# Scan stage: delta*u in PSUM, half scans, single-bank filters, and a GpSimd product that waits for its own state's scan alone

## Chip, cores and metric

The kernel runs on one core of a Trainium2 chip. The metric is the device time of one execution in microseconds (us), as the median of the runs.

## The reference

The network takes x of 16 sequences x 512 tokens x 128 features through six residual blocks: a mixture of experts, attention, two more mixtures, a selective state-space block, and a last mixture. The change touches the state-space block alone. Cut to what matters:

```python
xz = einsum('bld,ed->bel', h, W_in);  x, z = xz[:, :256], xz[:, 256:]
xc = gate[0] * silu(conv(x, w1, dil=1) + b1) + gate[1] * silu(conv(x, w2, dil=2) + b2)   # 4 taps each, causal
dt_low, B, C = split(W_x @ xc, [64, 16, 16])
delta = softplus(W_dt @ dt_low + b_dt);  A = -exp(A_log)             # A: 256 x 16 states
h_t = h_{t-1} * exp(delta_t * A) + delta_t * B_t * xc_t              # 512 steps, 256 x 16 states
y_t = sum over n of h_t[:, n] * C_t[n] + D * xc_t
out = W_out @ (y * silu(z))
```

## The kernel before

The kernel is a row of stages, with a barrier between them: load, routing, expert blocks (four times in all), attention, and `scan_stage` between the last two mixtures. Everything is float32 unless a row says bf16. X, all 8192 tokens, stays in SBUF throughout.

`scan_stage` goes through 16 sequences, and in each through NB = 16 states n. The 256 inner features lie as DT = 2 tiles of 128 partitions, so that one state is a tile of 128 x 1024 (2 x 512 time steps). Each engine runs a program of its own, written by hand: `run` calls `main(s, b, n)` and then `between(s, b, turn, n)` for each state. main is the recurrence of sequence s. between spreads the work of the neighbours over the states: the gating, the output projection, the residual and the routing of sequence s-1, the convolutions and step sizes of s+1, and the taking and the norm of s+2. Each engine executes its queue in order; semaphores (`wait_ge`) are the only ties.

For one state:
- ScalarE (`decay`) writes dA = exp(delta * A[n]) by two activations of 128 x 511 into a ring of RA = 4. In step n it makes state n+1.
- VectorE multiplies ux = delta*xc by the broadcast row B of the state, half by half (L1543, "mult A", and L1546, "mult B"), from SBUF into PSUM tile psX of three banks: even states use banks 0 and 1, odd ones 2 and 1, which is why the halves change places, (dt + n) % DT. Then one `tensor_tensor_scan` (L1552) runs over both halves, 1024 elements; the first dA of each half is 0 and so separates them. It writes H, a ring of RH = 4.
- GpSimd (L1484) multiplies H by the broadcast row C, both from SBUF, into HC, a ring of RP = 4. It waits for the scan of its state (h_ready), for both mults of the *next* state (dBx_done), and for TensorE to be done with the HC of three states before. For n < 8 it then issues one indirect DMA (L369) of a routed row block of sequence s-2.
- TensorE (`total`, L1310) adds HC to psY with an identity matmul, in step n+2.

On VectorE, between has after the scan of n = 1 the gating (L1529, one input in PSUM), after n = 3 the residual sum (L1534, one input in PSUM) and norm statistics (L148 to L158), after n = 5 the norm's end (L174 to L251), after n = 6 the sum and statistics of s+2 (L488, L148 to L156), after n = 9 their end (L174 to L181), after n = 10 the router's top (L299, L300) and `mix` (L1510), after n = 12 the router's choice (L315 to L328), after n = 14 the router's places (L345 to L349) and `step_sizes_1` (L1516), and after n = 15 `step_sizes_2` (L1520, L1521, L1523: delta and ux). Small operations in chains wait for the one before through semaphore `linked`.

TensorE's between has the convolutions of s+1 (`conv`, each 4 taps, g = 0 to 5) in PSUM tile psA of two banks, cut over steps 1 to 7 by CONV_STEPS, then `project` (n = 10) and `steps` (n = 12). ScalarE empties psA (`empty`), runs `silu` in n = 8 with two table loads, `to_low` in n = 11 and `soften` (softplus) in n = 13. SyncE writes the B and C rows to DRAM and loads them back broadcast, two states to a transfer, in four slots that wait for H*C.

PSUM: psA 2 banks, psX 3, psR 1, psY 2, all eight.

Of the kernel before, what the change touches and what calls it, by code (L numbers as in the profile page):

```python
# [19 lines left out]
P = 128  # L20
# [831 lines left out]
def attention_stage(nc, k, wqkv, source):  # L852


    with Stage(nc, "att") as st:
# [231 lines left out]
        def _(dve):  # L1087
# [37 lines left out]
            def body(s, b, turn, first, last):  # L1125
# [41 lines left out]
CONV_STEPS = {1: ((0, (0, 1)),), 2: ((0, (2, 3)),), 3: ((1, (0, 1, 2)),), 4: ((1, (3,)), (2, (0, 1))), 5: ((2, (2, 3)), (3, (0,))),  # L1167
              6: ((3, (1, 2, 3)),), 7: ((4, (0,)), (5, (0,)))}
EMPTY_STEPS = {2: (0,), 4: (1,), 5: (2,), 7: (3,), 8: (4, 5)}


def scan_stage(nc, k, source):
# [4 lines left out]
    with Stage(nc, "ssm") as st:  # L1177
# [6 lines left out]
        zs, xc, delta, ux = (sb(n, [P, 2, DT, SEQ]) for n in ("zs", "xc", "delta", "ux"))  # L1184
# [4 lines left out]
        ST, NB = SEQ_TILES, STATES  # L1189
        CHUNK, SLOTS = 2, 4  # L1190
# [3 lines left out]
        psA, psX = pb("psA", [P, 2, SEQ]), pb("psX", [P, DT + 1, SEQ])  # L1194
# [6 lines left out]
        dA_ready, dBx_done, h_ready, hc_ready, y_summed, y_ready, out_summed, added, cleared, z_done = map(  # L1201
            sem, "dA_ready dBx_done h_ready hc_ready y_summed y_ready out_summed added cleared z_done".split())
# [48 lines left out]
        def _(pe):  # L1251
            def flip(s):
                pe.wait_ge(normed, s + 1)
                if positive(s):
                    pe.wait_ge(v_ready, s)
                for j in range(ST):
                    last = nc.tensor.transpose(psA[:, 1, j * P:(j + 1) * P], xn[:, j, :], k.ident[:, :])
                last.then_inc(flipped, 1)

            def conv(s, g, taps=range(TAPS)):  # L1260

                c, dt = g // 2, g % 2
                o = psA[:, g % 2, :]
                if 0 in taps:
                    if g == 0:
                        pe.wait_ge(turned, s + 1)
                    if g >= 2:
                        pe.wait_ge(emptied, s * 6 + g - 1)
                if g < 2 * DT:
                    for t in taps:  # L1270
                        back = (TAPS - 1 - t) * (c + 1)
                        last = nc.tensor.matmul(o, Wtap[:, c, t, dt * P:(dt + 1) * P], hT[:, PAD - back:PAD - back + SEQ], start=(t == 0), stop=(t == TAPS - 1))  # L1272
                    done = TAPS - 1 in taps
                else:
                    last = nc.tensor.matmul(o, Win[:, INNER + dt * P:INNER + (dt + 1) * P], hT[:, PAD:PAD + SEQ], start=True, stop=True)
                    done = True
                if done:
                    last.then_inc(fronted, 1)
# [76 lines left out]
            steps(0)  # L1355
# [12 lines left out]
        def _(act):  # L1368
            def to_hT(s):
                act.wait_ge(flipped, s + 1)  # L1370
                nc.scalar.activation(hT[:, PAD:], psA[:, 1, :], ACT.Copy).then_inc(turned, 1)  # L1371

            def empty(s, b, g):
                c, dt = g // 2, g % 2
                act.wait_ge(fronted, s * 6 + g + 1)
                if g < 4:
                    nc.scalar.activation(pre[:, g, :], psA[:, g % 2, :], ACT.Identity, bias=col[:, dt, c:c + 1]).then_inc(emptied, 1)  # L1377
                else:
                    nc.scalar.activation(zs[:, b, dt, :], psA[:, g % 2, :], ACT.Copy).then_inc(emptied, 1)
# [10 lines left out]
            def to_low(s):  # L1390
# [309 lines left out]
```

## Time and profile before

| | us |
|---|---|
| median of 3 runs | 3390.18 (3386.60 to 3391.48) |
| the profiled execution | 3394.06 |
| its span in the profile | 3390.8 |
| scan stage in that span | about 1749 to 3012 |

Over the span TensorE is busy 2470.6 us (73%), VectorE 2227.6 (66%), GpSimd 1685.4 (50%) and ScalarE 1604.3 (47%). These shares mix stages with different limits, so the scan stage has to be read by itself. In a table of groups a line gives the source line, engine, operation, output <- inputs and shapes, the count, the busy time and the mean of one, and behind the bar the idle time in front and what ended it. In a list in order of time each line has start, duration (us), engine, source line and operation, and in brackets the idle time in front.

### The profile page before, as it was taken

Reading aid. Unit: us, or ns where it says so; the run is one execution under the profiler, and the core shown is the slowest. Engines: PE = TensorE matmul, PEld = TensorE weight load, DVE = VectorE, ACT = ScalarE, POOL = GpSimd, SP = SyncE. Lnnn points to the kernel's source line nnn. Section 1 sums busy time; section 2 is a strip of 40 time slices with the busy share of each in tenths; the row PEclk is TensorE's granted clock in tenths of the full one; section 3 lists DMA queues with packets and bytes.
Section 4 is the critical chain, followed back from the end, with each engine's and each line's share of the span. In section 5 each row is a group of like instructions: output and inputs, shape, how many; then the busy total and the mean of one; then the engine's idle time right before and its main releaser. Section 6 shows DMA issues by size and latency. Waiting matters only on the chain. (4 is left out here: it accounts for less than half of the span.)

```text
span 3390.8 us, 50612 instructions
## 1 busy us (share of the span) xinstructions
PE 2470.6 (73%) x12640; PEld 1752.9 (52%) x12640; DVE 2227.6 (66%) x6132; ACT 1604.3 (47%) x3126; POOL 1685.4 (50%) x1350
## 2 busy tenths in 40 slices
PE   2419995776499854499867777777777788739992
PEld 2319994555499833399723333333333333319992
DVE  3604445777444455255449999999999999974553
ACT  2205554454255433255445555555555555525551
POOL 2755550443455437555414555555555565654551
PEclk9999997777699976699978888888888888879996
DMA  8137871110478632477523333343333333317876
GB/s 289 52 99 229 226 209 47 54 57 28 120 229 226 175 105 85 132 229 226 167 88 112 120 123 113 118 133 113 125 113 113 125 118 116 120 57 231 225 228 177
DMA packets 268799, 478.94 MB, mean 141 GB/s; under 512 B 37453, under 2 KB 181803, under 8 KB 268560
## 3 DMA queue, kind: packets, MB, share of 16 engines
q1 hardware_dynamic: 208864, 388.64, 38.8%
q0 software_dynamic: 34816, 68.00, 5.6%
q10 hardware_dynamic: 25008, 21.11, 1.8%
q8 instruction: 35, 0.57, 0.1%
q14 instruction: 76, 0.62, 0.1%
HBM read 383.22 MB, written 98.54 MB: 142 GB/s over the span
## 5 line engine op out<-in xcount | busy, mean ns | idle before, releaser
L1484 POOL TENSOR_TENSOR ssm_HC<-ssm_H,ssm_BC 128x1024 f32<-128x1024 f32 x256 | 601.6, 2350 | 579.9 <-DVE ssm_psX L1546 532.3
L1310 PE MATMUL ssm_psY<-ssm_HC,ident 128*128 128x512 f32 x1024 | 555.1, 673 | 202.1 <-POOL ssm_HC L1484 201.5
L1552 DVE TENSOR_TENSOR_SCAN ssm_H<-ssm_dA,ssm_psX 128x1024 f32<-128x1024 f32 x256 | 585.3, 2286 | 44.7 <-issue 31.6
L1310 PEld LDWEIGHTS ssm_psY<-ssm_HC,ident 128*128 128x128 f32 x1024 | 205.1, 210 | 500.5 <-POOL ssm_HC L1484 272.9
L1419 ACT ACTIVATE ssm_dA<-ssm_delta,A 128x511 f32<-128x511 f32 x512 | 329.7, 708 | 102.9 <-DVE ssm_delta L1521 100.4
L369 POOL DMA_INDIRECT xslots<-att_r_xn,att_r_idx x128 | 127.9, 1000 | 246.5 <-DVE att_r_idx L349 210.4
L1272 PE MATMUL ssm_psA<-ssm_hT,Wtap 128*128 128x512 f32 x512 | 244.9, 613 | 2.5 <-ACT ssm_hT L1371 2.5
L768 POOL DMA_INDIRECT b_back<-b_yr,b_to_row x144 | 139.9, 972 | 151.1 <-DVE b_yr L843 129.2
L768 POOL DMA_INDIRECT a_back<-a_yr,a_to_row x144 | 139.9, 971 | 150.4 <-DVE a_yr L843 128.5
L768 POOL DMA_INDIRECT d_back<-d_yr,d_to_row x144 | 139.9, 972 | 148.6 <-DVE d_yr L843 126.7
L768 POOL DMA_INDIRECT c_back<-c_yr,c_to_row x144 | 139.9, 972 | 144.6 <-DVE c_yr L843 122.7
L1377 ACT ACTIVATE ssm_pre<-ssm_psA,col 128x512 f32<-128x512 f32 x64 | 43.7, 684 | 331.6 <-PE ssm_psA L1272 331.6
L1543 DVE TENSOR_TENSOR ssm_psX<-ssm_ux,ssm_BC 128x512 f32<-128x512 f32 x256 | 191.3, 747 | 9.2 <-issue 7.6
L812 ACT ACTIVATE d_H<-d_psH,d_W 128x256 f32<-128x256 f32 x288 | 127.5, 474 | 125.7 <-PE d_psH L789 125.7
L812 ACT ACTIVATE b_H<-b_psH,b_W 128x256 f32<-128x256 f32 x288 | 127.5, 474 | 125.4 <-PE b_psH L789 125.4
L812 ACT ACTIVATE c_H<-c_psH,c_W 128x256 f32<-128x256 f32 x288 | 127.5, 474 | 125.4 <-PE c_psH L789 125.4
L812 ACT ACTIVATE a_H<-a_psH,a_W 128x256 f32<-128x256 f32 x288 | 127.5, 474 | 124.7 <-PE a_psH L789 124.7
L812 ACT ACT_TABLE_LOAD x72 | 92.4, 1283 | 186.3 <-PEq L104 185.1
L1546 DVE TENSOR_TENSOR ssm_psX<-ssm_ux,ssm_BC 128x512 f32<-128x512 f32 x256 | 176.3, 689 | 0.0
L369 POOL DMA_INDIRECT xslots<-to_a_r_xn,to_a_r_idx x128 | 125.6, 981 | 97.6 <-DVE to_a_r_idx L349 56.6
L369 POOL DMA_INDIRECT xslots<-to_c_r_xn,to_c_r_idx x128 | 126.1, 985 | 90.6 <-DVE to_c_r_idx L349 49.8
L1272 PEld LDWEIGHTS ssm_psA<-ssm_hT,Wtap 128*128 128x128 f32 x512 | 101.9, 202 | 131.2 <-issue 127.9
(515 smaller groups left out, 5778.4 us busy)
## 6 DMA issues: line engine op xcount, KB each, us to landing
ssm_BC<-bc_rows SPq DMA_DIRECT2D x128, 1024.0 KB
a_W<-in_l_pack SPq DMA_DIRECT2D x72, 514.0 KB
b_W<-in_l_pack SPq DMA_DIRECT2D x72, 514.0 KB
c_W<-in_l_pack SPq DMA_DIRECT2D x72, 514.0 KB
d_W<-in_l_pack SPq DMA_DIRECT2D x72, 514.0 KB
a_xs<-xslots SPq DMA_DIRECT2D x72, 131.0 KB
b_xs<-xslots SPq DMA_DIRECT2D x72, 131.0 KB
c_xs<-xslots SPq DMA_DIRECT2D x72, 131.0 KB
```

What stands on the lines that cost most here:

```text
L369: pool.indirect_dma_start(out=self.k.xslots[:, :], out_offset=bass.IndirectOffsetOnAxis(ap=self.ids(s, b)[:, i:i + 1].bitcast(U32), axis=0 ...
L768: pool.indirect_dma_start(out=target[:, :], out_offset=bass.IndirectOffsetOnAxis(ap=to_row[:, q, s:s + 1].bitcast(U32), axis=0), in_=yr[:, ...
L812: nc.scalar.activation(H[:, b, f, :], psH[:, f, 0:BLOCK], gelu, bias=W[:, q, HIDDEN + FT * D + f:HIDDEN + FT * D + f + 1]).then_inc(h_read ...
L1272: last = nc.tensor.matmul(o, Wtap[:, c, t, dt * P:(dt + 1) * P], hT[:, PAD - back:PAD - back + SEQ], start=(t == 0), stop=(t == TAPS - 1))
L1310: last = nc.tensor.matmul(psY[:, dt, :], k.ident[:, :], HC[:, n % RP, (dt + n) % DT, :], start=False, stop=(n == NB - 1))
L1377: nc.scalar.activation(pre[:, g, :], psA[:, g % 2, :], ACT.Identity, bias=col[:, dt, c:c + 1]).then_inc(emptied, 1)
L1419: last = nc.scalar.activation(dA[:, n % RA, (dt + n) % DT, 1:], delta[:, b, dt, 1:], ACT.Exp, scale=A[:, dt, n:n + 1])
L1484: nc.gpsimd.tensor_tensor(HC[:, n % RP, :, :], H[:, n % RH, :, :], BC[:, n // CHUNK % SLOTS, 1, n % CHUNK:n % CHUNK + 1, :].to_broadcast([ ...
L1543: nc.vector.tensor_tensor(psX[:, 2 * odd, :], ux[:, b, 0, :], BC[:, c % SLOTS, 0, n % CHUNK, :], ALU.mult)
L1546: nc.vector.tensor_tensor(psX[:, 1, :], ux[:, b, 1, :], BC[:, c % SLOTS, 0, n % CHUNK, :], ALU.mult).then_inc(dBx_done, 1)
L1552: nc.vector.tensor_tensor_scan(flat(H[:, n % RH, :, :]), flat(dA[:, n % RA, :, :]), flat(psX[:, odd:odd + DT, :]), 0.0, ALU.mult, ALU.add) ...
```

## The change

1. `ux` moves from SBUF (two buffers) to PSUM (one, two banks). It is written for s+1 after n = 15, when the mults of s are done.
2. psX has two banks in place of three, and the halves no longer change places. Each half has a scan of its own of 512 elements, into its half of H. Scan A waits for mult A (new semaphore dBx_half), scan B for mult B. The next mult A waits for scan A (h_half), the next mult B for scan B.
3. GpSimd's H*C no longer waits for the mults of the next state.
4. psA has one bank in place of two. Each conv is whole in its step (g in step g+1) and waits for ScalarE to have emptied the one before; ScalarE empties g in step g+2. `steps` runs as two matmuls in n = 11 and 12, the second waiting for ScalarE's Relu of the first half, and `soften` in n = 12.
5. ScalarE makes dA two states ahead in place of one.
6. The taking of s+2 moves: TensorE's part from n = 4 to 0, VectorE's sum and statistics from n = 6 to 2. `out` of s-1 (TensorE, n = 2) waits for that sum, since both use psR.
7. The product with the diagonal D moves from the front of `total` (n = 0) to n = SKIP = 9.

```diff
-CONV_STEPS = {1: ((0, (0, 1)),), 2: ((0, (2, 3)),), 3: ((1, (0, 1, 2)),), 4: ((1, (3,)), (2, (0, 1))), 5: ((2, (2, 3)), (3, (0,))),
-              6: ((3, (1, 2, 3)),), 7: ((4, (0,)), (5, (0,)))}
-EMPTY_STEPS = {2: (0,), 4: (1,), 5: (2,), 7: (3,), 8: (4, 5)}
+CONV_STEPS = {1: 0, 2: 1, 3: 2, 4: 3, 5: 4, 6: 5}
+EMPTY_STEPS = {n + 1: g for n, g in CONV_STEPS.items()}
...
-        psA, psX = pb("psA", [P, 2, SEQ]), pb("psX", [P, DT + 1, SEQ])
+        psA, psX, ux = pb("psA", [P, SEQ]), pb("psX", [P, DT, SEQ]), pb("ux", [P, DT, SEQ])
...
+            def steps(s, dt):
+                if dt == 0:
+                    pe.wait_ge(low_ready, s + 1)
+                else:
+                    pe.wait_ge(v_half, s + 1)
+                nc.tensor.matmul(psA[:, :], Wdt[:, dt * P:(dt + 1) * P], low[0:RANK, :], start=True, stop=True).then_inc(dt_summed, 1)
 
             def out(s):
                 pe.wait_ge(y_ready, s + 1)
+                if there(s, 3):
+                    pe.wait_ge(G.taken, s + 4)
...
-                if n == 0:
-                    if positive(s):
-                        pe.wait_ge(y_ready, s)
+                if n == 0 and positive(s):
+                    pe.wait_ge(y_ready, s)
+                if n == SKIP:
                     for dt in range(DT):
-                        nc.tensor.matmul(psY[:, dt, :], diag[:, dt, :], xc[:, b, dt, :], start=True, stop=False)
+                        nc.tensor.matmul(psY[:, dt, :], diag[:, dt, :], xc[:, b, dt, :], start=False, stop=False)
...
             def soften(s):
-                act.wait_ge(dt_summed, s + 1)
...
+                    act.wait_ge(dt_summed, s * DT + dt + 1)
+                    nc.scalar.activation(absv[:, dt, :], psA[:, :], ACT.Abs, bias=col[:, dt, 2:3]).then_inc(abs_ready, 1)
+                    nc.scalar.activation(v[:, dt, :], psA[:, :], ACT.Relu, bias=col[:, dt, 2:3]).then_inc(v_half if dt == 0 else v_ready, 1)
...
             def main(s, b, n):
-                if n + 1 < NB:
-                    decay(s, b, n + 1)
+                if n + 2 < NB:
+                    decay(s, b, n + 2)
                 elif there(s, 1):
-                    decay(s + 1, 1 - b, 0)
+                    decay(s + 1, 1 - b, n + 2 - NB)
...
                 pool.wait_ge(h_ready, s * NB + n + 1)
-                if n + 1 < NB or there(s, 1):
-                    pool.wait_ge(dBx_done, s * NB + n + 2)
...
-                nc.vector.tensor_tensor(ux[:, b, :, :], delta[:, b, :, :], xc[:, b, :, :], ALU.mult).then_inc(ux_ready, 1)
+                if positive(s):
+                    dve.wait_ge(dBx_done, s * NB)
+                nc.vector.tensor_tensor(ux[:, :, :], delta[:, b, :, :], xc[:, b, :, :], ALU.mult).then_inc(ux_ready, 1)
...
-                odd = n % 2
-                nc.vector.tensor_tensor(psX[:, 2 * odd, :], ux[:, b, 0, :], BC[:, c % SLOTS, 0, n % CHUNK, :], ALU.mult)
+                if positive(s * NB + n):
+                    dve.wait_ge(h_half, s * NB + n)
+                nc.vector.tensor_tensor(psX[:, 0, :], ux[:, 0, :], BC[:, c % SLOTS, 0, n % CHUNK, :], ALU.mult).then_inc(dBx_half, 1)
                 if positive(s * NB + n):
                     dve.wait_ge(h_ready, s * NB + n)
-                nc.vector.tensor_tensor(psX[:, 1, :], ux[:, b, 1, :], BC[:, c % SLOTS, 0, n % CHUNK, :], ALU.mult).then_inc(dBx_done, 1)
-                dve.wait_ge(dBx_done, s * NB + n + 1)
+                nc.vector.tensor_tensor(psX[:, 1, :], ux[:, 1, :], BC[:, c % SLOTS, 0, n % CHUNK, :], ALU.mult).then_inc(dBx_done, 1)
+                dve.wait_ge(dBx_half, s * NB + n + 1)
                 dve.wait_ge(dA_ready, s * NB + n + 1)
                 if positive(s * NB + n - RH + 1):
                     dve.wait_ge(hc_ready, s * NB + n - RH + 1)
-                flat = lambda v: v.rearrange("p a t -> p (a t)")
-                nc.vector.tensor_tensor_scan(flat(H[:, n % RH, :, :]), flat(dA[:, n % RA, :, :]), flat(psX[:, odd:odd + DT, :]), 0.0, ALU.mult, ALU.add).then_inc(h_ready, 1)
+                nc.vector.tensor_tensor_scan(H[:, n % RH, 0, :], dA[:, n % RA, 0, :], psX[:, 0, :], 0.0, ALU.mult, ALU.add).then_inc(h_half, 1)
+                dve.wait_ge(dBx_done, s * NB + n + 1)
+                nc.vector.tensor_tensor_scan(H[:, n % RH, 1, :], dA[:, n % RA, 1, :], psX[:, 1, :], 0.0, ALU.mult, ALU.add).then_inc(h_ready, 1)
```

## Rows read from the trace of the kernel before

**Rows 1.** Busy time of each engine in a stretch: the scan stage.
```profile
core 0: us, PE busy (x) PEld busy (x) DVE busy (x) ACT busy (x) POOL busy (x), PEclk, DMA share, GB/s
1749.00:3012.00 1263.00, 970.67 (x2494) 424.48 (x2494) 1176.05 (x1729) 698.03 (x1110) 731.83 (x371) 0.87 0.34 116
```

**Rows 2.** Groups by line, scan stage: VectorE's scan and mult A, GpSimd's H*C.
```profile
L1552 DVE TENSOR_TENSOR_SCAN ssm_H<-ssm_dA,ssm_psX 128x1024 f32<-128x1024 f32 x256 | 585.3, 2286 | 44.7 <-issue 31.6 <-ACT ssm_dA L1419 1.8 <-DVE ssm_psX L1546 0.5
L1543 DVE TENSOR_TENSOR ssm_psX<-ssm_ux,ssm_BC 128x512 f32<-128x512 f32 x256 | 191.3, 747 | 9.2 <-issue 7.6 <-DVE ssm_ux L1523 0.2
...
L1484 POOL TENSOR_TENSOR ssm_HC<-ssm_H,ssm_BC 128x1024 f32<-128x1024 f32 x256 | 601.6, 2350 | 579.9 <-DVE ssm_psX L1546 532.3 <-issue 38.3 <-PE ssm_psY L1310 7.7
```

**Rows 3.** Waits, scan stage: who waited for whom; total us, times, longest.
```profile
POOL ssm_HC L1484 <- DVE ssm_psX L1546: 532.3, 175, 74.4
...
DVE ssm_H L1552 <- issue: 31.6, 17, 3.7
...
DVE ssm_v L1529 <- PE ssm_psY L1310: 9.3, 16, 4.5
```

**Rows 4.** VectorE in order of time: one state and the next mult A.
```profile
2401.60 0.69 DVE L1543 TENSOR_TENSOR ssm_psX<-ssm_ux,ssm_BC 128x512 f32<-128x512 f32 x1
2402.20 0.69 DVE L1546 TENSOR_TENSOR ssm_psX<-ssm_ux,ssm_BC 128x512 f32<-128x512 f32 x1
2402.93 2.29 DVE L1552 TENSOR_TENSOR_SCAN ssm_H<-ssm_dA,ssm_psX 128x1024 f32<-128x1024 f32 x1
2405.13 0.76 DVE L1543 TENSOR_TENSOR ssm_psX<-ssm_ux,ssm_BC 128x512 f32<-128x512 f32 x1
```

**Rows 5.** VectorE in order of time after the scan of n = 5.
```profile
2408.73 0.47 DVE L174 SCALAR_TENSOR_TENSOR ssm_r_newton<-ssm_r_root 128x8 f32<-128x8 f32 x1
2409.23 0.17 DVE L175 TENSOR_TENSOR ssm_r_newton<-ssm_r_newton,ssm_r_shifted 128x8 f32<-128x8 f32 x1
...
2409.90 0.42 DVE L248 TENSOR_SCALAR ssm_r_rstd<-ssm_r_rstd 128x4 f32<-128x4 f32 x1
```

**Rows 6.** GpSimd in order of time, beside rows 4 and 5.
```profile
2402.98 2.34 POOL L1484 TENSOR_TENSOR ssm_HC<-ssm_H,ssm_BC 128x1024 f32<-128x1024 f32 x1 [2.46 <-DVE ssm_psX L1546]
...
2406.79 2.37 POOL L1484 TENSOR_TENSOR ssm_HC<-ssm_H,ssm_BC 128x1024 f32<-128x1024 f32 x1
2409.32 1.01 POOL L369 DMA_INDIRECT xslots<-ssm_r_xn,ssm_r_idx  x1 [0.16 <-issue]
```

**Rows 7.** In order of time: GpSimd's H*C and VectorE's residual sum beside it.
```profile
2396.99 2.36 POOL L1484 TENSOR_TENSOR ssm_HC<-ssm_H,ssm_BC 128x1024 f32<-128x1024 f32 x1
...
2398.93 0.66 DVE L1534 TENSOR_TENSOR X<-X,ssm_psR 128x512 f32 x1
```

**Rows 8.** One line's instructions, ns min/median/max: L174 and L1484.
```profile
L174 DVE SCALAR_TENSOR_TENSOR ssm_r_newton<-ssm_r_root x16: 167/460/467, 1850.8 to 3018.1; 128x8 f32<-128x8 f32 x16
...
L1484 POOL TENSOR_TENSOR ssm_HC<-ssm_H,ssm_BC x256: 2332/2349/2377, 1755.7 to 3006.8; 128x1024 f32<-128x1024 f32 x128
```

**Rows 9.** VectorE in order of time after n = 3, n = 14 and n = 15.
```profile
2400.64 0.17 DVE L150 TENSOR_TENSOR ssm_r_mean<-ssm_r_stats 128x4 f32<-128x4 f32 x1
...
2400.99 0.17 DVE L153 TENSOR_SCALAR ssm_r_mean<-ssm_r_mean 128x4 f32<-128x4 f32 x1
...
2452.24 0.20 DVE L345 TENSOR_TENSOR ssm_r_pos<-ssm_psR,ssm_r_run 128x64 f32<-128x64 f32 x1
...
2452.57 0.21 DVE L347 TENSOR_TENSOR ssm_r_pos<-ssm_r_pos,ssm_r_hot 128x64 f32<-128x64 f32 x1
...
2457.94 1.26 DVE L1520 TENSOR_TENSOR ssm_rest<-ssm_pre,ssm_rest 128x1024 f32<-128x1024 f32 x1
2459.24 1.23 DVE L1521 TENSOR_TENSOR ssm_delta<-ssm_rest,ssm_v 128x1024 f32<-128x1024 f32 x1
```

**Rows 10.** ScalarE in order of time: the decays behind the silu block.
```profile
2429.77 2.54 ACT L1419 ACTIVATE ssm_dA<-ssm_delta,A 128x511 f32<-128x511 f32 x4
```

**Rows 11.** Groups by line, VectorE after the last state: a scan of 8.
```profile
L404 DVE TENSOR_TENSOR_SCAN ssm_r_end<-ssm_r_ones,ssm_r_nblk 128x8 f32<-128x8 f32 x1 | 0.2, 175 | 0.0
```

**Rows 12.** TensorE in order of time: a part of the convs, and totals after a wait.
```profile
2411.34 2.74 PE L1272 MATMUL ssm_psA<-ssm_hT,Wtap 128*128 128x512 f32 x6
...
2448.90 5.56 PE L1310 MATMUL ssm_psY<-ssm_HC,ident 128*128 128x512 f32 x8 [2.45 <-POOL ssm_HC L1484]
```

More of the change, by code:

```diff
@@ L1256, in flip, with conv @@
                 for j in range(ST):
[L1257 removed]
+                    last = nc.tensor.transpose(psA[:, j * P:(j + 1) * P], xn[:, j, :], k.ident[:, :])
                 last.then_inc(flipped, 1)
[L1260 removed]
+            def conv(s, g):
                 c, dt = g // 2, g % 2
[L1263 to L1268, printed above, removed]
+                if g == 0:
+                    pe.wait_ge(turned, s + 1)
+                else:
+                    pe.wait_ge(emptied, s * 6 + g)
                 if g < 2 * DT:
[L1270 removed]
+                    for t in range(TAPS):
                         back = (TAPS - 1 - t) * (c + 1)
[L1272 to L1278 removed]
+                        last = nc.tensor.matmul(psA[:, :], Wtap[:, c, t, dt * P:(dt + 1) * P], hT[:, PAD - back:PAD - back + SEQ], start=(t == 0), stop=(t == TAPS - 1))
+                else:
+                    last = nc.tensor.matmul(psA[:, :], Win[:, INNER + dt * P:INNER + (dt + 1) * P], hT[:, PAD:PAD + SEQ], start=True, stop=True)
+                last.then_inc(fronted, 1)
             def project(s, b):
@@ L1325, in between @@
                     if n == 7:
-                        if there(s, 2):
-                            pe.wait_ge(G.taken, s + 3)
+                        pe.wait_ge(added, s)
                         R.pe_1a(nc, pe, s - 1, 1 - b)
@@ L1333, in between @@
                 if there(s, 1):
-                    for g, taps in CONV_STEPS.get(n, ()):
-                        conv(s + 1, g, taps)
+                    if n in CONV_STEPS:
+                        conv(s + 1, CONV_STEPS[n])
                     if n == 10:
                         project(s + 1, 1 - b)
+                    if n == 11:
+                        steps(s + 1, 0)
                     if n == 12:
-                        steps(s + 1)
+                        steps(s + 1, 1)
                 if there(s, 2):
-                    if n == 4:
-                        if there(s, -1):
-                            pe.wait_ge(added, s)
+                    if n == 0:
+                        if there(s, -2):
+                            pe.wait_ge(R.rowed, s - 1)
                         G.pe(nc, pe, s + 2, b, turn + 1, psR)
@@ L1370, in to_hT @@
                 act.wait_ge(flipped, s + 1)
-                nc.scalar.activation(hT[:, PAD:], psA[:, 1, :], ACT.Copy).then_inc(turned, 1)
+                nc.scalar.activation(hT[:, PAD:], psA[:, :], ACT.Copy).then_inc(turned, 1)
             def empty(s, b, g):
@@ L1438, in between @@
                 if there(s, 1):
-                    for g in EMPTY_STEPS.get(n, ()):
-                        empty(s + 1, 1 - b, g)
+                    if n in EMPTY_STEPS:
+                        empty(s + 1, 1 - b, EMPTY_STEPS[n])
                     if n == 0:
```

40 lines of the change are left out of this document (17 added, 23 removed).

## Prediction

> **What bounds the kernel now.** I read the busy table by stretch first, then the groups by line, then the waits, then single instructions in order of time. In the scan stage (1749 to 3012 us) VectorE is busy 1176 of 1263 us, TensorE 971, GpSimd 732, ScalarE 698 [rows 1]. VectorE's own idle there is small: 31.6 us before 17 scans ("issue"; behind them, a late dA from ScalarE) and 9.3 us before 16 gated multiplies [rows 3]. So the stage is as long as VectorE's queue, and the change counts by what it does to that queue. GpSimd's H*C idles 532 us, nearly all of it in the wait that the change removes [rows 3]; that idle costs nothing by itself. The other stages are not touched.
>
> One state n costs VectorE 0.60 us from mult A (L1543) to mult B (L1546), 0.73 to the scan (L1552), 2.20 to the next instruction: 3.53 [rows 4]. The 0.73 holds a drain: the scan waits for mult B, which ended at 2402.89. Next instructions otherwise start about 0.09 before the last one's end.
>
> **The fact on which all turns.** Before, GpSimd's H*C (2.35 us, and none of 256 shorter than 2.33 or longer than 2.38 [rows 2, 8]) starts when mult B of the next state has ended, and so runs beside a scan. Where it ran over the scan's end, the VectorE instruction behind was held. At 2408.73 the 128x8 L174 (two inputs in SBUF) took 0.47 us instead of the 0.17 of its neighbour L175, and ended at 2409.20; the H*C beside it ended at 2406.79 + 2.37 = 2409.16 [rows 5, 6]. Its median over 16 sequences is 0.460 [rows 8]. The same H*C tails lift mult A to a mean of 0.747 [rows 2]. On the other hand L1534, with one input in PSUM, started at 2398.93 with the H*C of 2396.99 still running to 2399.35, and took 0.66 [rows 7]; and the scans (dA in SBUF, psX in PSUM) run beside H*C throughout. So in this trace H*C holds back VectorE instructions with both inputs in SBUF and no others. The longest hold seen is about 0.3 us, since by design none of them starts earlier under an H*C. That it would be the whole rest of an H*C is my step beyond the rows. For it: the held L174 got nothing done until the H*C was over (it ended 0.04 us after it), and in 256 H*C none gave way by as much as 0.03 us. GpSimd's indirect DMA holds a third kind: tensor_scalar L248, 0.42 us, ended 2410.32, the DMA at 2410.33 [rows 5, 6].
>
> The Trainium skill ("SBUF — State Buffer", section "Who interferes with whom") says the same of the kinds and more of the length: VectorE with two SBUF inputs and a GpSimd instruction that reads SBUF exclude each other, and whoever is first keeps the port for its whole instruction. The kinds and the tails agree, with L174's 0.47 us; the length of a whole instruction no row here shows. By the rule the sum comes out as the forecast below, by the tails alone as rival 1.
>
> **The change, part by part.**
>
> *ux in PSUM, free mults.* With ux in PSUM, mult A and B have one SBUF input and should pass H*C like L1534. This removes 0.747 - 0.690 = 0.057 us per state.
>
> *Half scans.* Scan A waits for mult A alone, so the drain behind mult B goes: 0.73 becomes 0.60, -0.13. Two scans cost one more fixed part. A scan of 8 elements takes 0.175 [rows 11], one of 1024 2.286 [rows 2]: 2.08 ns an element and 0.16 fixed, so a half is 1.22 and, less the overlap of 0.09, 1.13; twice is 2.27 against 2.20: +0.07. Per state -0.057 - 0.13 + 0.07 = -0.12; x256 = **-31 us**. A mult from PSUM to PSUM isn't in the trace. Bounds: no added cost for the second scan (-0.19, -49 us) to a full fixed part of 0.175 for it and for a slower PSUM mult, with nothing gained (+0.30, +77 us). I take -31, since L1534's 0.66 is nearest.
>
> *dA two states ahead.* dA of a state behind the silu block is the first half of the pair of decays that starts at 2429.77 [rows 10] and is done 1.27 later, at 2431.04, when the waiting scan starts (one of the 17 of rows 3). One more state of lead (3.5 us) covers the 1.6 us of each of 15 waits: **-25 us**, leaving the start of the stage. Soften moves from n=13 to 12 and has its chain through one bank, TensorE waiting for Relu and ScalarE for TensorE; its results are wanted at n=14 and 15, so I cost it at nothing; were the cover gone, one matmul pair and one activation, some 1.5 us a sequence, 25 us.
>
> *TensorE.* Convs at n=1 to 4 are whole: 8 records of 0.43 (six took 2.74 with the last one's tail) = 3.44, with total 1.72, 5.2 us a step [rows 12], against VectorE's 3.5 plus what stands between. At n=2, out now waits for the dve_sum of n=2 (G.taken); total(1) and the convs queue behind it. total(n-2) is wanted only by H*C of n+1 at the earliest and that by a scan three later, so lag of two or three states is hidden: nothing. diag at n=9 rather than n=0 is the same work. SP's loads follow H*C, which comes earlier, not later: nothing.
>
> *H*C free.* This is the large term. H*C now starts about 0.09 after its own scan's end (as 2402.98 follows 2402.89), and so 0.18 after the first instruction that stands between this state and the next starts. What stands there (between) has both inputs in SBUF in 8 of 16 places, and was run in peace before. If a held instruction waits to the H*C's end:
> - n=9: L174 is in front, H*C slips in behind it and L175 waits nearly 2.35. n=5 the same. 2.35 each.
> - n=14: L347 starts 0.33 after the first, so 2.35 - (0.33 - 0.18) = 2.20 is left [rows 9]. n=10 (mix L1510) and n=12 (L316) lie between 2.20 and 2.35. n=15: H*C begins when L1520 ends, L1521 waits 2.35 [rows 9]. These four: 9.1.
> - n=2 and n=3: L150 comes 1.71 after the PSUM sum (2398.93 to 2400.64): 2.35 - (1.71 - 0.18) = 0.82 left. Then the indirect DMA (0.16 later, 1.01 long) meets tensor_scalar L153, 0.35 after L150: again 0.82 [rows 6, 7, 9]. 1.64 each.
>
> With 15 sequences for n=3, 5, 10, 12, 14, 15 and 14 for n=2 and 9: 15 x (1.64 + 2.35 + 9.1) + 14 x (1.64 + 2.35) = 196 + 56 = **+252 us**. Gone in return are the old tails before L174, 32 x 0.30 = **-9**, and about half of the gated wait, **-4**.
>
> Sum: -31 - 25 - 9 - 4 + 252 = **+183 us**. Profiled span 3390.8 gives 3574; that execution took 3394.1, 3.9 over the median of 3390.2, so the median to be expected is **3573 us**.
>
> **The rivals.**
> 1. *The hold is only a tail, or VectorE keeps ahead* (no whole-instruction hold; or H*C doesn't get in between chained instructions, whose gaps are 0.03 to 0.05 us). For: no row shows a hold over 0.4 us. Against: each held instruction ended with the H*C, and no H*C was ever lengthened. Then the 252 is about 0 and the time is 3390 - 69 = **3321 us**, faster. The point from which it decides: the gains of 69 us over 15 x 6 + 14 x 2 = 118 places are 0.58 us a place; with shorter holds than that the kernel is faster. Chance 0.15.
> 2. *A part of it*: the short chained instructions keep H*C out and only the two places with long ones (n=10, 15) are held, 15 x 4.6 = 69, or half of all holds come, 126: 3321 + 69 to 126 = **3390 to 3447**. Chance 0.10.
> 3. *TensorE becomes the bound, beside the holds.* From n=1 to 4 it has 4 x 3.44 of convs, three totals of 1.72 and some 1.9 of out: 21 us at full clock, against 24 of VectorE with its holds. But the granted clock averages 0.87 [rows 1], and after a wait eight records took 5.56 instead of 3.44 [rows 12]. At that pace the 21 become 34, 10 too many; the ring of four H*C hides three states, 10 us, so it decides only where the lag has begun before. If half of the 10 comes through, 15 x 5 = 75: **3648**. Chance 0.06.
> 4. The forecast: holds in full, **3573**. Chance 0.69. Its own range is 3510 to 3640: a quarter of the holds less on the one side; on the other a third of the +108 us that the upper state bound lies above the value taken, and the 25 of soften.
>
> The range is 3400 to 3640: it leaves out rivals 1 and 3. About 0.2% (7 us) is what can be told from no change: faster 0.17, same 0.03, slower 0.80.
>
> **What would show it.** Right: L175 at n=5 and 9, L316 or L317, L347, L1510, L1521 with durations or idle near 2.4 us that end with an H*C; mult A at 0.69 with an H*C running; mult A, mult B, scan A and scan B spaced 0.60, 0.60, 1.13 and 1.13; a sequence 11 to 12 us longer; VectorE still the longest queue; the wait of scan 10 gone. Wrong: those instructions at 0.2 us beside a running H*C; or mults stretched beside it (then ux in PSUM doesn't free them, and the time is over 3640); or scans waiting for dA or hc_ready, which would name ScalarE or TensorE.

## The result, and the profile after

| | before | after |
|---|---|---|
| median, us | 3390.67 (4 runs) | 3532.39 (4 runs, 3530.83 to 3534.42) |
| ratio | | 1.0421, 95% interval 1.0403 to 1.0439 |
| span of the profiled execution | 3390.8 | 3529.0 |
| scan stage, from the start of the first H*C to that of the last gated multiply | 1255.5 | 1391.1 |

The kernel is 142 us slower; 183 were forecast. Nearly all of it is in the scan stage: 1391.1 - 1255.5 = 135.6 of the 138.2 us of the span. The executions come from several chips, and the kernel before takes 3501 to 3538 us on some of them. What is longer there lies outside the scan stage: the kernel of the first experiment below has a stage of 1199.9 us on one chip and 1198.6 on another, and 2292.2 and 2136.7 us outside it; why, no run tells. So below I give the ratio to the kernel before on the same chip, and the length of the scan stage as in the last line of the table. Each stage length is read from one trace; the two pairs of traces of one kernel (1199.9 and 1198.6, 1391.1 and 1390.7) differ by up to 1.3 us, so less than that can't be told from nothing.

The busy time of each engine over the stage, after (columns as in rows 1):

```profile
1749.00:3152.00 1403.00, 1003.66 (x2495) 433.57 (x2496) 1350.51 (x2001) 708.54 (x1112) 733.38 (x373) 0.86 0.31 105
```

VectorE is busy 1350.5 of 1403 us, against 1176.1 of 1263 [rows 1]. It is still the bound, and what grew is its busy time, not its idle time: an instruction that is held counts as busy. The groups by line, VectorE, scan stage (count, busy us, mean ns; behind the bar the idle time before):

```profile
L1551 DVE TENSOR_TENSOR_SCAN ssm_H<-ssm_dA,ssm_psX 128x512 f32<-128x512 f32 x255 | 308.3, 1209 | 0.8 <-issue 0.8
L1553 DVE TENSOR_TENSOR_SCAN ssm_H<-ssm_dA,ssm_psX 128x512 f32<-128x512 f32 x255 | 304.3, 1193 | 0.0
L1543 DVE TENSOR_TENSOR ssm_psX<-ssm_ux,ssm_BC 128x512 f32<-128x512 f32 x255 | 178.5, 700 | 18.3 <-issue 16.3 <-DVE ssm_ux L1522 1.4
...
L1518 DVE TENSOR_TENSOR ssm_delta<-ssm_rest,ssm_v 128x1024 f32<-128x1024 f32 x15 | 48.7, 3245 | 0.5
L1507 DVE SCALAR_TENSOR_TENSOR ssm_xc<-ssm_pre,gates,ssm_xc 128x1024 f32<-128x1024 f32 x15 | 47.2, 3148 | 0.0
L316 DVE TENSOR_TENSOR ssm_r_work<-ssm_r_prob,ssm_r_pv 128x32 f32<-128x32 f32 x30 | 38.3, 1276 | 1.0
L175 DVE TENSOR_TENSOR ssm_r_newton<-ssm_r_newton,ssm_r_shifted 128x8 f32<-128x8 f32 x15 | 37.6, 2507 | 0.5
L347 DVE TENSOR_TENSOR ssm_r_pos<-ssm_r_pos,ssm_r_hot 128x64 f32<-128x64 f32 x15 | 34.0, 2270 | 0.0
L175 DVE TENSOR_TENSOR ssm_n_newton<-ssm_n_newton,ssm_n_shifted 128x4 f32<-128x4 f32 x14 | 33.0, 2357 | 0.5
...
L150 DVE TENSOR_TENSOR ssm_r_mean<-ssm_r_stats 128x4 f32<-128x4 f32 x15 | 12.7, 850 | 0.5
L150 DVE TENSOR_TENSOR ssm_n_mean<-ssm_n_stats 128x4 f32<-128x4 f32 x14 | 11.8, 840 | 0.5
```

Nearly all of the growth is at the places that the prediction named. L175 multiplies 128 x 8 numbers and takes 2.51 us, where its neighbours take 0.17. Above what each takes when nothing holds it (1.225 for L1518, 1.274 for L1507, 0.192 for L316, 0.167 and 0.162 for L175, 0.215 for L347, 0.166 for L150), the eight lines from L1518 down lost 30.3 + 28.1 + 32.5 + 35.1 + 30.8 + 30.7 + 10.3 + 9.4 = 207 us, and L158, L251 and L1513, which it had not named, another 5 or so: 212 us.

One such place in order of time, VectorE and then GpSimd, after n = 9 (start, duration in us):

```profile
2410.85 0.13 DVE L174 SCALAR_TENSOR_TENSOR ssm_n_newton<-ssm_n_root 128x4 f32<-128x4 f32 x1
2411.02 2.36 DVE L175 TENSOR_TENSOR ssm_n_newton<-ssm_n_newton,ssm_n_shifted 128x4 f32<-128x4 f32 x1
2413.41 0.16 DVE L176 SCALAR_TENSOR_TENSOR ssm_n_rstd<-ssm_n_newton,ssm_n_root 128x4 f32<-128x4 f32 x1
...
2411.01 2.35 POOL L1481 TENSOR_TENSOR ssm_HC<-ssm_H,ssm_BC 128x1024 f32<-128x1024 f32 x1 [0.76 <-DVE ssm_H L1553]
```

H*C comes 0.03 us after L174's end, in the gap of the chain, and L175 ends at 2413.38, 0.02 after the H*C. (At n = 5 an indirect DMA runs in front of the H*C, and L175 starts 0.13 us before the H*C does; it is held all the same, for 2.50 to 2.53 us, and for 2.36 in the one sequence that has no DMA there.) Compare rows 5 and 6, where L174 was held for the last 0.3 us of an H*C only. After n = 15 it also goes the other way:

```profile
2447.32 1.20 DVE L1517 TENSOR_TENSOR ssm_rest<-ssm_pre,ssm_rest 128x1024 f32<-128x1024 f32 x1
2448.55 3.25 DVE L1518 TENSOR_TENSOR ssm_delta<-ssm_rest,ssm_v 128x1024 f32<-128x1024 f32 x1
...
2447.48 3.24 POOL L1481 TENSOR_TENSOR ssm_HC<-ssm_H,ssm_BC 128x1024 f32<-128x1024 f32 x1 [5.31 <-DVE ssm_H L1553]
```

L1517 was first, and the H*C takes 3.24 us instead of 2.35 since it has to wait for L1517; then L1518 waits for the H*C.

A state with nothing behind it, VectorE; with rows 4 beside it one sees the half scans and the free mults:

```profile
2400.60 0.67 DVE L1543 TENSOR_TENSOR ssm_psX<-ssm_ux,ssm_BC 128x512 f32<-128x512 f32 x1
2401.18 0.68 DVE L1546 TENSOR_TENSOR ssm_psX<-ssm_ux,ssm_BC 128x512 f32<-128x512 f32 x1
2401.78 1.21 DVE L1551 TENSOR_TENSOR_SCAN ssm_H<-ssm_dA,ssm_psX 128x512 f32<-128x512 f32 x1
2402.91 1.19 DVE L1553 TENSOR_TENSOR_SCAN ssm_H<-ssm_dA,ssm_psX 128x512 f32<-128x512 f32 x1
2404.02 0.67 DVE L1543 TENSOR_TENSOR ssm_psX<-ssm_ux,ssm_BC 128x512 f32<-128x512 f32 x1
...
2400.77 2.35 POOL L1481 TENSOR_TENSOR ssm_HC<-ssm_H,ssm_BC 128x1024 f32<-128x1024 f32 x1 [3.49 <-DVE ssm_H L1553]
```

The spacings are 0.58, 0.60, 1.13 and 1.11, together 3.42, with an H*C running beside mult B and most of mult A.

### The profile page after: what moved, and what is told of

The parts are those of the page before. It is cut to its first block and busy times, and to the rows that moved or that the text cites. A ratio compares the mean times of both kernels' runs of the same rounds, so it can differ in the third digit from the quotient of the medians.

```text
span 3529.0 us, 51026 instructions
## 1 busy us (share of the span) xinstructions
PE 2505.1 (71%) x12640; PEld 1759.0 (50%) x12640; DVE 2398.8 (68%) x6388; ACT 1614.5 (46%) x3126; POOL 1683.9 (48%) x1350
## 5 line engine op out<-in xcount | busy, mean ns | idle before, releaser
L1481 POOL TENSOR_TENSOR ssm_HC<-ssm_H,ssm_BC 128x1024 f32<-128x1024 f32 x256 | 616.6, 2409 | 720.2 <-DVE ssm_H L1553 711.0
L1551 DVE TENSOR_TENSOR_SCAN ssm_H<-ssm_dA,ssm_psX 128x512 f32<-128x512 f32 x256 | 309.5, 1209 | 2.6 <-ACT ssm_dA L1416 1.8
L1553 DVE TENSOR_TENSOR_SCAN ssm_H<-ssm_dA,ssm_psX 128x512 f32<-128x512 f32 x256 | 305.5, 1193 | 0.0
L1543 DVE TENSOR_TENSOR ssm_psX<-ssm_ux,ssm_BC 128x512 f32<-128x512 f32 x256 | 179.2, 700 | 18.3 <-issue 16.3
L1546 DVE TENSOR_TENSOR ssm_psX<-ssm_ux,ssm_BC 128x512 f32<-128x512 f32 x256 | 176.0, 688 | 0.0
```

What stands on the lines that cost most here:

```text
L1481: nc.gpsimd.tensor_tensor(HC[:, n % RP, :, :], H[:, n % RH, :, :], BC[:, n // CHUNK % SLOTS, 1, n % CHUNK:n % CHUNK + 1, :].to_broadcast([ ...
L1543: nc.vector.tensor_tensor(psX[:, 0, :], ux[:, 0, :], BC[:, c % SLOTS, 0, n % CHUNK, :], ALU.mult).then_inc(dBx_half, 1)
L1546: nc.vector.tensor_tensor(psX[:, 1, :], ux[:, 1, :], BC[:, c % SLOTS, 0, n % CHUNK, :], ALU.mult).then_inc(dBx_done, 1)
L1551: nc.vector.tensor_tensor_scan(H[:, n % RH, 0, :], dA[:, n % RA, 0, :], psX[:, 0, :], 0.0, ALU.mult, ALU.add).then_inc(h_half, 1)
L1553: nc.vector.tensor_tensor_scan(H[:, n % RH, 1, :], dA[:, n % RA, 1, :], psX[:, 1, :], 0.0, ALU.mult, ALU.add).then_inc(h_ready, 1)
```

## The experiments

Two theories stood at the start. Theory H: the time goes into holds, as above. Theory T: it goes into TensorE's filters in one bank and its new waits, which the holds only accompany. The next four ran on one chip.

**The wait put back.**

```diff
                 pool.wait_ge(h_ready, s * NB + n + 1)
+                if n + 1 < NB or there(s, 1):
+                    pool.wait_ge(dBx_done, s * NB + n + 2)
```

> The changed kernel with GpSimd's wait for the mults of the next state put back, all else as changed. Theory H (H*C holds VectorE's instructions with two SBUF inputs to its own end): the 212 us that the held instructions lost go, 3532 - 212 = 3320 us, L175 back at 0.17, mix at 1.27, H*C beside the scans. Rival T (the loss comes from TensorE's one-bank filters or from its new waits on the taking of s+2): these are still in, so it stays at 3500 or more.

Measured: 0.9854 of before (0.9838 to 0.9871), stage 1199.9 us: 191 less than the changed kernel, and 56 less than the kernel before. Two more of its lines, VectorE's groups in the scan stage:

```profile
L1545 DVE TENSOR_TENSOR ssm_psX<-ssm_ux,ssm_BC 128x512 f32<-128x512 f32 x254 | 175.1, 689 | 10.3 <-issue 8.2 <-DVE ssm_ux L1524 1.4
...
L174 DVE SCALAR_TENSOR_TENSOR ssm_n_newton<-ssm_n_root 128x4 f32<-128x4 f32 x14 | 10.1, 724 | 0.0
```

Theory T falls: its parts are all still in. The 21 us that are missing from the expected 212 are mostly tails (the last part of an H*C, which runs on past the scan's end and holds the next instruction). They come back with the wait: L174 at n = 9 has a mean of 0.72 in place of 0.14. And the gated multiply waits for TensorE's totals for 13.4 us in all in place of 6.3. The whole account stands in the part on the prediction.

**ux in SBUF, H*C free.**

```diff
+        ux = sb("ux", [P, DT, SEQ])
...
-        psA, psX, ux = pb("psA", [P, SEQ]), pb("psX", [P, DT, SEQ]), pb("ux", [P, DT, SEQ])
+        psA, psX = pb("psA", [P, SEQ]), pb("psX", [P, DT, SEQ])
```

> The changed kernel with ux back in SBUF (one buffer), H*C still free. Theory H: the mults have two SBUF inputs again, so mult A is held after n = 0, 4, 6, 7, 8, 11, 13 by some 2.2 us and after n = 1 by about 1; 16.3 us a sequence more, 3532 + 260 = 3790 us, mult A's mean near 1.7. Rival (the place of ux is nothing to H*C): within 10 us of 3532, mult A near 0.70.

Measured: 3958 us, against 3538 before on that chip (one execution), stage 1672.5 us: 281 more than the changed kernel, 260 expected. VectorE's groups:

```profile
L1547 DVE TENSOR_TENSOR ssm_psX<-ssm_ux,ssm_BC 128x512 f32<-128x512 f32 x255 | 434.5, 1704 | 0.0
...
L1544 DVE TENSOR_TENSOR ssm_psX<-ssm_ux,ssm_BC 128x512 f32<-128x512 f32 x255 | 204.5, 802 | 18.9 <-issue 16.8 <-DVE ssm_ux L1523 1.4
```

The size was right, the place was not: mult B is held (1.70 us), not mult A. Mult A starts 0.09 us before the scan ends and so before H*C can; H*C gets in behind it. So ux in PSUM does what it is for: with a free H*C it is worth 280 us.

**dA two states ahead, alone, in the kernel before.**

```diff
-                if n + 1 < NB:
-                    decay(s, b, n + 1)
+                if n + 2 < NB:
+                    decay(s, b, n + 2)
                 elif there(s, 1):
-                    decay(s + 1, 1 - b, 0)
+                    decay(s + 1, 1 - b, n + 2 - NB)
...
             decay(0, 0, 0)
+            decay(0, 0, 1)
```

> The kernel before with dA made two states ahead, that one part alone. If ScalarE's silu block was what scan 10 waited for: 25 us less, 3365 us, and the idle time before the scans nearly gone. If the late dA has another cause: 3390, with the idle time moved to another n.

Measured: 0.9905 (0.9889 to 0.9922), stage 1224.8: 30.7 us less. The scan's group has 11.4 us of idle time in front, and no "issue" in it, in place of 44.7 with 31.6 [rows 2]:

```profile
L1553 DVE TENSOR_TENSOR_SCAN ssm_H<-ssm_dA,ssm_psX 128x1024 f32<-128x1024 f32 x255 | 583.0, 2286 | 11.4
```

**The wait put back and ux in SBUF** (both edits above).

> The changed kernel with the wait put back and ux in SBUF. Theory H: ux in PSUM is then worth only the tails, since H*C starts behind the mults: 0.057 x 256 = 15 us above the kernel that has the wait alone, 3335 us, mult A at a mean of 0.75. If PSUM as a source has a gain or a price of its own, the two differ by more, or the other way.

Measured: 0.9923 (0.9906 to 0.9939), stage 1222.9. That is 23.0 us more than with the wait alone, where 15 were expected: mult A's mean is 0.804, not 0.75. With half scans the second scan ends 2.23 us after mult B (median; 2.32 in the kernel before), while H*C, which starts 0.13 after mult B's end in both, ends 2.35 later: the tail is longer than it was.

**Half scans alone, in the kernel before.** This and the next three ran on a second chip.

```diff
-                nc.vector.tensor_tensor(psX[:, 2 * odd, :], ux[:, b, 0, :], BC[:, c % SLOTS, 0, n % CHUNK, :], ALU.mult)
+                nc.vector.tensor_tensor(psX[:, 2 * odd, :], ux[:, b, 0, :], BC[:, c % SLOTS, 0, n % CHUNK, :], ALU.mult).then_inc(dBx_half, 1)
...
-                dve.wait_ge(dBx_done, s * NB + n + 1)
+                dve.wait_ge(dBx_half, s * NB + n + 1)
...
-                flat = lambda v: v.rearrange("p a t -> p (a t)")
-                nc.vector.tensor_tensor_scan(flat(H[:, n % RH, :, :]), flat(dA[:, n % RA, :, :]), flat(psX[:, odd:odd + DT, :]), 0.0, ALU.mult, ALU.add).then_inc(h_ready, 1)
+                nc.vector.tensor_tensor_scan(H[:, n % RH, odd, :], dA[:, n % RA, odd, :], psX[:, 2 * odd, :], 0.0, ALU.mult, ALU.add)
+                dve.wait_ge(dBx_done, s * NB + n + 1)
+                nc.vector.tensor_tensor_scan(H[:, n % RH, 1 - odd, :], dA[:, n % RA, 1 - odd, :], psX[:, 1, :], 0.0, ALU.mult, ALU.add).then_inc(h_ready, 1)
```

> The kernel before with the scan cut into two of 512, the first waiting for mult A alone; that one part. From mult B to the scan 0.60 in place of 0.73, the two scans 2.24 to 2.27 in place of 2.20, and mult A's tail 0.05 longer, since H*C still starts behind mult B: 0.01 to 0.05 us a state gained, 3 to 13 us, 0.996 to 0.999 times before. If the second scan costs a full fixed part with no overlap, it is slower than before by 20 us or more.

Measured: 1.0005 (0.9996 to 1.0015), stage 1254.3: 1.2 us less, no difference, where 3 to 13 us were expected. The two scans gain the drain and lose most of it to the second start; mult A's longer tail (0.794 in place of 0.748, 46 ns x 256 = 12 us) takes the rest.

**H*C as two instructions, free.**

```diff
-                nc.gpsimd.tensor_tensor(HC[:, n % RP, :, :], H[:, n % RH, :, :], BC[:, n // CHUNK % SLOTS, 1, n % CHUNK:n % CHUNK + 1, :].to_broadcast([P, DT, SEQ]), ALU.mult).then_inc(hc_ready, 1)
+                nc.gpsimd.tensor_tensor(HC[:, n % RP, 0, :], H[:, n % RH, 0, :], BC[:, n // CHUNK % SLOTS, 1, n % CHUNK, :], ALU.mult)
+                nc.gpsimd.tensor_tensor(HC[:, n % RP, 1, :], H[:, n % RH, 1, :], BC[:, n // CHUNK % SLOTS, 1, n % CHUNK, :], ALU.mult).then_inc(hc_ready, 1)
```

> The changed kernel with H*C as two instructions of 512 elements, one for each half, still free. Theory H, a hold for the whole of one GpSimd instruction: each hold is some 1.2 us in place of 2.35; between the two halves the held VectorE instruction gets its turn, and a chain (L316, L317) is then held a second time by the second half, 1.2 us each; mix, which has no chain behind it, loses 1.2 us less. So 17 to 30 us under the changed kernel, 1.033 to 1.037 times before. If the hold were a slowing down while both run, mix would keep its 3.15 us and the sum of L316 and L317 would be as now.

Measured: 1.0321 (1.0302 to 1.0340), stage 1362.4, 28.7 us under the changed kernel, though 11.6 of these 28.7 are a cost of the loop that the expectation didn't have (below, "One cost I had not seen"). In order of time, VectorE and GpSimd, after n = 12:

```profile
2511.26 1.28 DVE L316 TENSOR_TENSOR ssm_r_work<-ssm_r_prob,ssm_r_pv 128x32 f32<-128x32 f32 x1
2512.57 1.19 DVE L317 TENSOR_TENSOR ssm_r_work<-ssm_r_work,small 128x32 f32<-128x32 f32 x1
...
2511.22 1.26 POOL L1481 TENSOR_TENSOR ssm_HC<-ssm_H,ssm_BC 128x512 f32<-128x512 f32 x1 [0.92 <-DVE ssm_H L1554]
2512.45 1.26 POOL L1482 TENSOR_TENSOR ssm_HC<-ssm_H,ssm_BC 128x512 f32<-128x512 f32 x1
```

L316 is held by the first half, gets its turn at once when it ends, and L317 is held by the second. Mix (L1508), a single long instruction, has a mean of 2.12 in place of 3.15, and the second half of H*C waits for it (2.25 us instead of 1.26). So at these places what is held is held for one GpSimd instruction, and a slowing down of both is excluded: L316, mix and L317 lengthen by their waits.

But it isn't so at all places. At n = 5 L175 has a mean of 2.70 in this kernel, more than with the whole H*C:

```profile
2040.39 2.81 DVE L175 TENSOR_TENSOR ssm_r_newton<-ssm_r_newton,ssm_r_shifted 128x8 f32<-128x8 f32 x1
...
2040.66 1.28 POOL L1481 TENSOR_TENSOR ssm_HC<-ssm_H,ssm_BC 128x512 f32<-128x512 f32 x1
2041.89 1.28 POOL L1482 TENSOR_TENSOR ssm_HC<-ssm_H,ssm_BC 128x512 f32<-128x512 f32 x1
```

L175 started 0.27 us before the first half, beside an indirect DMA, and got no turn between the halves. And after n = 14 one input in SBUF was enough to be held: L349 copies 128 x 8 numbers to int32, and in all 15 sequences it took 0.88 in place of 0.17 beside the second half, and ended 0.02 after it:

```profile
2174.26 0.88 DVE L349 CAST ssm_r_idx<-ssm_r_row 128x8 int32<-128x8 f32 x1
...
2173.85 1.27 POOL L1482 TENSOR_TENSOR ssm_HC<-ssm_H,ssm_BC 128x512 f32<-128x512 f32 x1
```

L148 (BATCH_NORM_STATS2) and L348 (TENSOR_REDUCE), also with one input in SBUF, were not held by more than 0.02 us.

**The wait at the eight places only, and at the other eight only.**

```diff
+                if n in (2, 3, 5, 9, 10, 12, 14, 15) and (n + 1 < NB or there(s, 1)):
+                    pool.wait_ge(dBx_done, s * NB + n + 2)
```

The second has `n not in`.

> The changed kernel with the wait for the next state's mults put back only after n = 2, 3, 5, 9, 10, 12, 14 and 15, where VectorE has instructions with two SBUF inputs between two states; free elsewhere. Theory H: as good as the wait everywhere, and some 10 us better, since the tails before L174 at n = 5 and 9 go: 0.982 times before. If a free H*C costs something of its own elsewhere (a price on the mults or scans), it is above 0.985.

Measured: 0.9861 (0.9846 to 0.9877), stage 1200.9: as good as the wait everywhere, and not better.

> The opposite: the wait only after n = 0, 1, 4, 6, 7, 8, 11 and 13, free at the eight places. Theory H: nearly as slow as the changed kernel; only the hold at n = 5 shrinks, since H*C of n = 4 and its DMA now run late and H*C of n = 5 comes behind L175. Scan stage 1391 - 30 = 1361 us, 1.03 times before. If the number of free H*C is what counts and not their place, it is halfway, 1.01.

Measured: 1.0520 (1.0504 to 1.0536), stage 1427.6, 36 us *more* than the changed kernel. My size was wrong, and its sign: I had looked at L175 at n = 5 alone. The wait at n - 1 makes the H*C in front late, the next one starts in the middle of the chain or follows the late one at once, and may hold an instruction for longer. VectorE and GpSimd, n = 5:

```profile
2515.09 0.32 DVE L174 SCALAR_TENSOR_TENSOR ssm_r_newton<-ssm_r_root 128x8 f32<-128x8 f32 x1
...
2515.84 3.12 DVE L181 SCALAR_TENSOR_TENSOR ssm_r_shift<-ssm_r_mean,ssm_r_rstd 128x4 f32<-128x4 f32 x1
...
2516.58 2.36 POOL L1483 TENSOR_TENSOR ssm_HC<-ssm_H,ssm_BC 128x1024 f32<-128x1024 f32 x1
```

L175 was past, as expected, and L181 is held in its place, until 2518.96 (H*C ends at 2518.94). It had started 0.74 us before the H*C, during the indirect DMA of n = 4 (2515.54 to 2516.55), so it was held across both. At n = 9 L174 starts under a late H*C and isn't let in before the next:

```profile
2252.21 2.92 DVE L174 SCALAR_TENSOR_TENSOR ssm_n_newton<-ssm_n_root 128x4 f32<-128x4 f32 x1
...
2250.45 2.37 POOL L1483 TENSOR_TENSOR ssm_HC<-ssm_H,ssm_BC 128x1024 f32<-128x1024 f32 x1
2252.76 2.35 POOL L1483 TENSOR_TENSOR ssm_HC<-ssm_H,ssm_BC 128x1024 f32<-128x1024 f32 x1
```

So a held instruction isn't sure of the next turn: it can lose the rest of one GpSimd instruction and the whole of the one behind it. In what these places differ from L316 and L317 above, which took turns with the halves, no run settles. At n = 2, L150 now takes 2.24 us in most sequences (mean 2.00 in place of 0.84), 16 of the 36 us. Still, with both runs together the place decides: the eight H*C that the first of the two leaves free cost nothing (1200.9 us against 1199.9), and no instruction with two SBUF inputs comes right behind them.

**Lag, and a faster kernel.** Three kernels on a third chip: the changed one again, the one with the wait put back again, and one that has the wait put back and spreads GpSimd's DMAs over the states:

```diff
-                if n < 8 and there(s, -2):
-                    R.pool_one(pool, s - 2, b, n)
+                if n % 2 == 0 and there(s, -2):
+                    R.pool_one(pool, s - 2, b, n // 2)
```

> The changed kernel itself, beside the next two on one chip. The scan stage at 1391 us as in its first trace, and 191 us more than with the wait back. On a chip on which the kernel before takes 3500 to 3540 us, the same 140 us more are a ratio of 1.040.

> The changed kernel with the wait put back, once more, on the same chip as the changed kernel and the spread DMAs: scan stage 1200 us, 0.985 times before.

> The changed kernel with the wait put back, and GpSimd's eight indirect DMAs of a sequence issued after every second state (n = 0, 2, ... 14) rather than after n = 0 to 7. With the DMA (0.17 + 1.01 us) behind it an H*C takes GpSimd 3.53 us, and VectorE's state is now 3.42, so H*C lags behind through n = 4 to 8 and its tail holds L174 at n = 5 (0.47 in place of 0.14) and at n = 9 (0.77). Spread, the lag goes: L174 at 0.15 to 0.25, 10 to 14 us under the kernel with the wait alone, some 0.982 times before. If the tails only move to another held instruction, no difference from it.

Measured on one chip, with the kernel before at 3389.37: the changed kernel 1.0423 (1.0407 to 1.0439), 3533 us, stage 1390.7; with the wait back 0.9858 (0.9843 to 0.9873), 3340 us, stage 1198.6; with the DMAs spread as well 0.9835 (0.9822 to 0.9849), 3335 us, stage 1194.4. The spread is worth 4 to 5 us, not 10 to 14: L174 at n = 5 and 9 still takes 0.32, not 0.15 to 0.25, and L316 takes 1.5 us more. The instructions of L174 at n = 9 in these two kernels (ns min/median/max), first with the wait alone, then with the DMAs spread:

```profile
L174 DVE SCALAR_TENSOR_TENSOR ssm_n_newton<-ssm_n_root x16: 161/764/839, 1693.7 to 2782.9; 128x4 f32<-128x4 f32 x16
```

```profile
L174 DVE SCALAR_TENSOR_TENSOR ssm_n_newton<-ssm_n_root x16: 161/312/368, 1696.8 to 2779.7; 128x4 f32<-128x4 f32 x16
```

The lag from the DMAs was real: 0.45 of the 0.62 by which L174 was over its own 0.14. What is left, 0.17, goes when the H*C of n = 4 and 8 are free as well:

> The spread DMAs together with the wait at the eight places only, so that the H*C of n = 4 and 8 are free and over before L174 of n = 5 and 9. Theory H: L174 loses its last 0.17 us, 30 x 0.17 = 5 us under the spread DMAs alone: 0.982 times before, L174 at 0.14. If the tail stays at 0.31, the H*C in front is late for another reason than its start behind the mults, and the ratio is 0.9835 as with the spread DMAs alone.

Measured: 0.9837 (0.9820 to 0.9854), stage 1192.2, with

```profile
L174 DVE SCALAR_TENSOR_TENSOR ssm_n_newton<-ssm_n_root x16: 134/136/164, 1832.4 to 2911.3; 128x4 f32<-128x4 f32 x16
```

L174 is at its 0.14, as theory H has it; the 5 us that were expected in the time did not show (this one ran on a fourth chip, and a stage 2 us shorter can't be told from the spread DMAs alone). The kernel with the spread DMAs is 54 us faster than the kernel before and 198 us faster than the changed one, on the same chip.

## Why the prediction was right, and where its sizes were off

The parts, from runs that differ in one of them (the fourth row is what is left over), in us of the scan stage:

| part | forecast | measured | from |
|---|---|---|---|
| dA two ahead | -25 | -30.7 | 1224.8 - 1255.5 |
| half scans | -15 | -1.2 | 1254.3 - 1255.5 |
| ux in PSUM, with the wait | -15 | -23.0 | 1199.9 - 1222.9 |
| TensorE, soften, the moved taking and the rest | 0 | -0.7 | 1222.9 - (1255.5 - 30.7 - 1.2) |
| H*C free | +252 - 13 | +191.2 | 1391.1 - 1199.9 |
| sum | +183 | +135.6 | |

- **The bound and the hold.** That VectorE's queue sets the stage, that an H*C holds two-input instructions to its end, and that it slips into the gaps of a chain, all came as written. The step beyond the rows, from a tail of 0.3 us to a whole 2.35, is now shown, by L175 at 2.36 us.
- **How far the rule goes.** The Trainium skill ("SBUF — State Buffer", section "Who interferes with whom") agrees with the traces in three points: a hold lasts for the whole instruction (L175, 2.36 us), either side can be first (the 3.24 us H*C), and a multiply with one SBUF input is free (mult A, 0.67 beside an H*C). That whoever is first keeps the port does not cover what came at n = 5 and 9 of the last pair of runs, where L181 and L174 had been waiting and the H*C that began later was served before them (3.12 and 2.92 us). The prediction's "both inputs in SBUF and no others" was true of the trace that it read, and is too narrow: the int32 copy L349 has one.
- **Luck.** Without the free H*C the forecast is -31 - 25 = -56 us, and the measured 1199.9 - 1255.5 is -55.6. The agreement is luck: the half scans gain 14 less than forecast, ux in PSUM 8 more and dA 6 more.
- **The term that was too large** is the holds: 252 forecast, 212 measured. 24 us of it is L153: I had the indirect DMA hold a tensor_scalar for the DMA's whole length. It doesn't (below); L158 and L251 lost some 4 us instead. Another 21 us, spread over the eight lines, is the start-up of a held instruction, which passes while it waits: mix ends 1.08 us after the H*C, not 1.27 (over 2.20 forecast, 1.87 measured), L175 at n = 9 lost 2.20 in place of 2.35, L150 0.68 in place of 0.82. 24 and 21, less the 5 us of the lines that weren't named, make the 40.
- **Against that**, 191 is less than 212 because the comparison kernel keeps tails (L174 13 us, L248 3) and gated waits (7 us) and 5 us of late dA, which the free H*C does away with; the 8 us of the loop (below) go the other way. That the tails go (9 forecast) was right.
- **The state.** 3.53 to 3.42, 0.11 gained, by the isolated spacings; forecast 0.12. But the two halves of this weren't what I wrote: half scans gain nothing by themselves, ux in PSUM gains more. With ux in SBUF the shorter scans also lengthen the tail of H*C under mult A, which the forecast had put at nothing. And the forecast's upper bound of a state doesn't add up: two fixed parts of 0.175 with nothing gained are +0.35 (90 us), not +0.30 (77); the range hardly moves by it.
- **dA.** Six us more than forecast, as the start of the stage (3.7 and 1.7 us of waits there) gained too, which I had left out.
- **One cost I had not seen:** at each of the four back jumps of VectorE's loop (after every second sequence) the first mult A starts late, by 1.9 us before and 4.1 after ("issue", 7.6 and 16.3 us in the groups by line); with the wait put back it is 8.2 in all. No H*C is running at that time (in one case it ended 6.8 us before, at 2177.72, while the mult starts at 2184.48). The 8 us come with a whole H*C that is free after n = 15: they are there in the two other kernels that have one (16.8 and 16.9 us) and not where the wait stands at n = 15 (8.0), and with the H*C in two halves it is only 4.7. Why stays open; no run was made on it.
- **The rivals.** Rivals 1 and 2 (tail only, a part of it) are excluded by the durations, rival 3 (TensorE) by the changed kernel's idle time, where VectorE waits 6.3 us for TensorE in the whole stage, and by the stage with the wait put back.

## What to carry to other kernels

When GpSimd works on SBUF beside a VectorE that is the bound, list every VectorE instruction that can start under a GpSimd one, not only the large ones in the inner loop: two multiplications of 128 x 8 and 128 x 4 numbers (L175) lost 66 us, where ux in PSUM gains 23 with the wait in place. Moving one operand to PSUM frees a multiply, and a wait on GpSimd that looks like idle time may be what protects the rest; give GpSimd its start where what follows has been seen to run beside it (here multiplies and scans with an input in PSUM, norm statistics, reductions), and check the others one by one (here a copy to int32 was held). A GpSimd instruction that starts late can cost more than one that starts early, if the next stands right behind it. Held time counts as busy, so look at means that differ from those of neighbours of the same size.

## What the runs showed of the hardware that I had not expected

An indirect DMA on GpSimd with nothing right behind it holds a VectorE tensor_scalar only in its later part. VectorE and GpSimd, changed kernel, after n = 5:

```profile
2396.65 0.17 DVE L248 TENSOR_SCALAR ssm_r_rstd<-ssm_r_rstd 128x4 f32<-128x4 f32 x1
2396.87 0.40 DVE L251 TENSOR_SCALAR ssm_r_xn<-token 128x4 f32 x1
...
2396.27 1.01 POOL L369 DMA_INDIRECT xslots<-ssm_r_xn,ssm_r_idx  x1 [0.17 <-issue]
```

L248, 0.38 us after the DMA's start, runs freely in 0.17; L251, 0.60 after it, is held until 2397.27, and the DMA ends at 2397.28. Before, L248 came 0.58 after the DMA's start and was held [rows 5, 6]. So two forms of GpSimd work hold in different ways: H*C from its start, the DMA from some point between 0.38 and 0.58 us on. With an H*C right behind the DMA it is earlier: with the wait at the other eight places only, L181 (two inputs in SBUF) was held from 0.30 us after the DMA's start in 13 of 14 sequences, where it ran freely at the same 0.30 in the kernel before.

And a scan cut in two costs little: 1.209 + 1.193 us for the halves, which overlap by 0.08, against 2.286 for the whole. A held instruction can be passed by the next GpSimd instruction, and a copy to int32 with one input in SBUF can be held: both stand with the experiments above.
